# Round 0's gathered rows passed through TensorE into PSUM, its queries moved within a turn, and the last chunk of a round stored in pieces

## What is computed

```python
e   = relu((x[dst] - x[src]) @ theta_w.T + theta_b + x[src] @ phi_w.T + phi_b)
x   = layernorm(x + segment_max(e, dst))            # empty nodes: 0
hv  = x @ W_in + b_in
for W, b in ((W_u0, b_u0), (W_u1, b_u1)):
    m  = relu(concat(hv[src], he) @ W + b)
    hv = where(has_in, segment_max(m, dst) + hv, hv)
out = layernorm(x + relu(hv @ W_ro + b_ro))
```

## Time and profile before

| what | value |
|---|---|
| median of 3 runs | 3306.88 us (3306.12 to 3308.51) |
| the profiled execution | 3308.03 us |
| its span, first to last instruction | 3306.2 us |
| busy: POOL / PE / DVE / ACT | 2416.1 / 2101.3 / 1463.1 / 186.1 us |
| mean granted clock of TensorE | 0.831 of full speed (full: 2.4 GHz) |
| DMA | 770.03 MB, mean 233 GB/s |

### The profile page before, as it was taken

One profiled execution on the slowest core, in us unless ns is written; L12 is line 12 of the kernel. 1 busy time (PEld: TensorE's weight loads), 2 busy tenths in 40 slices (PEclk: granted clock), 3 DMA queues, 4 the chain that ended last, 5 costly groups with the idle time before them and its releaser, 6 DMA issues.

```text
span 3306.2 us, 21987 instructions
## 1 busy us (share of the span) xinstructions
PE 2101.3 (64%) x5442; PEld 1052.2 (32%) x5442; DVE 1463.1 (44%) x3430; ACT 186.1 (6%) x422; POOL 2416.1 (73%) x2536
## 2 busy tenths in 40 slices
PE   5322221222221888788787887778888888888867
PEld 4211111111110633333333333353343344333435
DVE  2655555555554733333333333323333333333337
ACT  1000000000000600000000000010000000000005
POOL 4777777777776677777777777667777777777765
PEclk8655555555555999999999999989999999999999
DMA  7666666666665767777777777677777777777764
GB/s 255 209 215 224 224 223 224 224 225 220 211 217 193 235 221 245 247 241 239 244 242 245 239 249 246 220 252 243 246 245 251 254 247 246 248 259 245 245 209 151
DMA packets 265661, 770.03 MB, mean 233 GB/s; under 512 B 55443, under 2 KB 114686, under 8 KB 227902
## 3 DMA queue, kind: packets, MB, share of 16 engines
q0 software_dynamic: 122208, 334.92, 33.5%
q1 hardware_dynamic: 84478, 354.64, 28.4%
q10 hardware_dynamic: 58848, 79.06, 8.0%
HBM read 421.22 MB, written 347.19 MB: 232 GB/s over the span
## 4 chain that ended last, share of the span: by engine, by line
POOL 47%; DMA 17%; issue 16%; PE 15%; DVE 3%; ACT 1%; DVEq 0%; ACTq 0%; POOLq 0%; SPq 0%
POOL gath L525 45%; DMA gath<-table,src_sb 16%; PE edge_ps L746 6%; PE edge_ps L744 4%; PE side_ps L685 2%; POOL gath L552 2%; PE edge_ps L685 2%; DVE hist L356 1%; DMA gath<-runs,end_row 1%; DVE hist L393 1%; ACT gath L636 0%; DMA runs<-hist 0%; ACT hist L623 0%; ACT x_sb L636 0%; DMA table<-hist 0%
## 5 line engine op out<-in xcount | busy, mean ns | idle before, releaser
L525 POOL DMA_INDIRECT gath<-table,src_sb x2352 | 2244.4, 954 | 767.0 <-issue 668.8
L356 DVE SCALAR_TENSOR_TENSOR hist<-hist,lift,edge_ps 128x256 f32<-128x256 f32 x1568 | 752.7, 480 | 1229.5 <-PE edge_ps L746 1167.9
L746 PE MATMUL edge_ps<-gath,ident 128*128 128x512 f32 x1568 | 852.3, 626 | 343.0 <-DMA gath<-table,src_sb 342.3
L744 PE MATMUL edge_ps<-w_e,he_sb 128*128 128x512 f32 x1568 | 817.7, 603 | 1.0 <-DVE hist L416 0.5
L693 PE MATMUL edge_ps<-dst_f,onehot 128*128 128x512 f32 x200 | 145.5, 881 | 731.9 <-DVE onehot L281 731.9
L356 DVE SCALAR_TENSOR_TENSOR hist<-hist,lift,gath 128x256 f32<-128x256 f32 x784 | 381.2, 486 | 426.1 <-DMA gath<-table,src_sb 382.5
L746 PEld LDWEIGHTS edge_ps<-gath,ident 128*128 128x128 f32 x1568 | 284.1, 194 | 808.4 <-DMA gath<-table,src_sb 553.3
L744 PEld LDWEIGHTS edge_ps<-w_e,he_sb 128*128 128x128 f32 x1568 | 298.5, 196 | 349.4 <-issue 333.9
L693 PEld LDWEIGHTS edge_ps<-dst_f,onehot 128*128 128x128 f32 x200 | 57.7, 318 | 809.4 <-DVE onehot L281 759.0
L595 ACT COPY hv_sb<-side_ps 128x256 f32<-128x256 f32 x147 | 54.7, 372 | 2884.0 <-PE edge_ps L746 1865.1
L552 POOL DMA_INDIRECT gath<-runs,end_row x147 | 151.7, 1032 | 49.0 <-issue 43.6
(11 more groups left out here) (125 smaller groups left out, 904.9 us busy)
## 6 DMA issues: line engine op xcount, KB each, us to landing
runs<-hist SPq DMA_DIRECT2D x294, 1024.0 KB, 5.2
he_sb<-in_he ACTq DMA_DIRECT2D x196, 256.0 KB, 3.0
gath<-table,src_sb POOLq DMA_INDIRECT x2352, 3.3
table<-hist SPq DMA_DIRECT2D x72, 256.0 KB, 3.5
back_T<-x1T ACTq DMA_DIRECT2D x98, 128.0 KB, 3.3
back_T<-in_xT ACTq DMA_DIRECT2D x49, 128.0 KB, 2.5
x_sb<-in_x SPq DMA_DIRECT2D x49, 128.0 KB, 4.9
back_T<-msgT ACTq DMA_DIRECT2D x49, 128.0 KB, 5.8
```

The costliest lines, as they stand in the source:

```text
L356: state = V.scalar_tensor_tensor(hist[:, s % H, :], hist[:, (s - 1) % H, :], lift[:, t:t + 1], edges, ALU.add, ALU.max)
L525: pool.indirect_dma_start(gath[:, s % G, :], None, tables[r], bass.IndirectOffsetOnAxis(src_sb[:, t:t + 1], 0)).then_inc(gathered[s % G // ...
L744: T.matmul(bank, he_sb[:, c % NHE, at:at + P], w_e[r - 1][:, :], start=True, stop=False)
L746: last = T.matmul(bank, ident[:, :], flat(gath[:, s % G:s % G + 2, :]), start=False, stop=True)
```

## The change

- **Rows through PE.** A new function `first_rows` takes the place of PE's round 0 loop. For each pair of steps PE waits for both gathers and multiplies the rows with the identity into one PSUM bank. DVE reads from the bank in all rounds. Round 0 uses three banks (0 to 2), so PE is at most 6 steps ahead of DVE; rounds 1 and 2 keep six.
- **Ring release.** In round 0 POOL's wait for a free slot of `gath` is now on `group_summed` (PE) instead of `state_done` (DVE).
- **Queries early.** `pick_rows` moves from step 8 of a turn to step 0, PE's `pick` stands after the second group, `find_ends` after step 7 instead of after step 15. `back` stands after the third group. `multiply_weights` stands after the sixth group of turn 1 and uses the two query banks and a side bank; `weights_and_biases` stands ahead of step 32 instead of behind step 47.
- **Store in pieces.** The last chunk of each round goes out as four DMAs of two steps (256 KB) instead of one of eight (1 MB). `stores(n)` counts the DMAs of a chunk's slot.

```diff
-EDGE_BANKS = 6
+EDGE_BANKS = (3, 6, 6)
+WEIGHTS_AT = (LATE_TURN + 1) * BODY
+        weights_ps = [edge_ps[:, BANKS, :], edge_ps[:, BANKS + 1, :], side_ps[:, 0, :]]
+        edge_bank = lambda r, t: edge_ps[:, t // 2 % EDGE_BANKS[r], :]
+        def stores(n):
+            return sum(SC // GS if m % CHUNKS == CHUNKS - 1 else 1 for m in range(n % NS, n + 1, NS))
             def edge_maxima(r):
-                    if r == 0 and t % BODY == BODY // 2:
+                    if r == 0 and t == WEIGHTS_AT:
+                        weights_and_biases()
+                    if r == 0 and t % BODY == 0:
                         pick_rows(col_no[:, :])
                     if s % SC == 0 and s >= H:
-                        dve.wait_ge(stored[s // SC % NS], 16 * (s // H))
-                    if r == 0 and s % 2 == 0:
-                        dve.wait_ge(gathered[s % G // 2], 2 * 16 * (s // G + 1))
-                    elif r > 0 and s % GS == 0:
-                        dve.wait_ge(group_summed, s // GS - GROUPS + 1)
+                        dve.wait_ge(stored[s // SC % NS], 16 * stores(s // SC - NS))
+                    if s % GS == 0:
+                        dve.wait_ge(group_summed, s // GS + 1)
                     V.drain()
-                    edges = gath[:, s % G, :] if r == 0 else edge_ps[:, bank, half:half + D]
+                    edges = edge_bank(r, t)[:, t % 2 * D:(t % 2 + 1) * D]
...
-                    if r == 0 and t % BODY == BODY - 1:
+                    if r == 0 and t % BODY == BODY // 2 - 1:
...
-                        if i == LATE_TURN + 1:
-                            weights_and_biases()
             def store_runs(r):
-                    sp.wait_ge(state_done, (n + 1) * SC // GS)
-                    at = n % NS * SC
-                    sp.dma_start(runs_by_part[:, c * SC:(c + 1) * SC, :], hist[:, at:at + SC, :]).then_inc(stored[n % NS], 16)
+                    piece = GS if c == CHUNKS - 1 else SC
+                    for t in range(c * SC, (c + 1) * SC, piece):
+                        s = r * STEPS + t
+                        sp.wait_ge(state_done, (s + piece) // GS)
+                        sp.dma_start(runs_by_part[:, t:t + piece, :], hist[:, s % H:s % H + piece, :]
+                                     ).then_inc(stored[n % NS], 16)
             def gather_edges(r):
-                    if s % GS == 0 and G <= s < STEPS + G:
-                        pool.wait_ge(state_done, (s - G) // GS + 1)
-                    elif s % GS == 0 and s >= G:
-                        pool.wait_ge(group_summed, (s - G) // GS - GROUPS + 1)
+                    if s % GS == 0 and s >= G:
+                        pool.wait_ge(group_summed, (s - G) // GS + 1)
+            def first_rows():
+                for g in range(GROUPS):
+                    turn_no, at = g // (BODY // GS), g % (BODY // GS) * GS
+                    if g == 0:
+                        pe.wait_ge(product_out, NU)
+                    if g * GS >= 2 * EDGE_BANKS[0]:
+                        pe.wait_ge(state_done, g - 2 * EDGE_BANKS[0] // GS + 1)
+                    for t in range(g * GS, (g + 1) * GS, 2):
+                        pe.wait_ge(gathered[t % G // 2], 2 * 16 * (t // G + 1))
+                        last = T.matmul(edge_bank(0, t), ident[:, :], flat(gath[:, t % G:t % G + 2, :]),
+                                        start=True, stop=True)
+                    last.then_inc(group_summed, 1)
+                    if at == GS:
+                        pick(turn_no + 1)
+                    if at == BODY // 4:
+                        for t in back_tiles(0, turn_no):
+                            back(t)
+                    if turn_no == LATE_TURN and at == BODY // 2 + GS:
+                        multiply_weights()
...
                 if r == 0:
-                    for i in range(TURNS):
-                        for t in back_tiles(0, i):
-                            back(t)
-                        pick(i + 1)
-                        if i == LATE_TURN:
-                            multiply_weights()
+                    first_rows()
```

More of the change, by code:

```diff
@@ L133, in gnn_kernel @@
         assert 2 * XT_BUFS <= G and 2 * (ROW_BUFS + UNIT_BUFS) <= G and 4 * UNIT_BUFS <= H
-        edge_ps = ctx.enter_context(nc.psum_tensor("edge_ps", [P, EDGE_BANKS, 2 * D], f32))
+        edge_ps = ctx.enter_context(nc.psum_tensor("edge_ps", [P, max(EDGE_BANKS), 2 * D], f32))
         side_ps = ctx.enter_context(nc.psum_tensor("side_ps", [P, 2, 2 * D], f32))
@@ L319, in weights_and_biases @@
                 dve.wait_ge(weights_mult, 1)
-                for n, w in enumerate((w_in_n0, w_in_n1, w_in_ro)):
-                    V.tensor_copy(flat(w[:, :, :]), edge_ps[:, n, :])
+                for w, w_ps in zip((w_in_n0, w_in_n1, w_in_ro), weights_ps):
+                    V.tensor_copy(flat(w[:, :, :]), w_ps)
                 for n, b_ps in ((NEXT0, edge_ps[:, 3, 0:D]), (NEXT1, edge_ps[:, 3, D:]), (OUT, side_ps[:, 1, 0:D])):
@@ L344, in edge_maxima @@
                     s = r * STEPS + t
-                    if r == 0 and t % BODY == BODY // 2:
+                    if r == 0 and t == WEIGHTS_AT:
+                        weights_and_biases()
+                    if r == 0 and t % BODY == 0:
                         pick_rows(col_no[:, :])
                     if s % SC == 0 and s >= H:
-                        dve.wait_ge(stored[s // SC % NS], 16 * (s // H))
-                    if r == 0 and s % 2 == 0:
-                        dve.wait_ge(gathered[s % G // 2], 2 * 16 * (s // G + 1))
-                    elif r > 0 and s % GS == 0:
-                        dve.wait_ge(group_summed, s // GS - GROUPS + 1)
+                        dve.wait_ge(stored[s // SC % NS], 16 * stores(s // SC - NS))
+                    if s % GS == 0:
+                        dve.wait_ge(group_summed, s // GS + 1)
                     V.drain()
-                    bank, half = s // 2 % EDGE_BANKS, s % 2 * D
-                    edges = gath[:, s % G, :] if r == 0 else edge_ps[:, bank, half:half + D]
+                    edges = edge_bank(r, t)[:, t % 2 * D:(t % 2 + 1) * D]
                     state = V.scalar_tensor_tensor(hist[:, s % H, :], hist[:, (s - 1) % H, :], lift[:, t:t + 1], edges,
@@ L530, in join_partitions @@
                 for n in range((r + 1) * CHUNKS - NS, (r + 1) * CHUNKS):
-                    pool.wait_ge(stored[n % NS], 16 * (n // NS + 1))
+                    pool.wait_ge(stored[n % NS], 16 * stores(n))
                 if r == 0:
@@ L580, in load_he @@
                 if n >= NHE:
-                    act.wait_ge(group_summed, (n - NHE + 1) * HC // GS)
+                    act.wait_ge(group_summed, GROUPS + (n - NHE + 1) * HC // GS)
                 act.dma_start(he_sb[:, n % NHE, :], a["he"][:, c * HC // 2 * P:(c + 1) * HC // 2 * P]
@@ L724, in multiply_weights @@
                         for h in range(KH):
-                            T.matmul(edge_ps[:, n, m * D:(m + 1) * D], w_inT[:, h, m * P:(m + 1) * P], w[:, h, :],
+                            T.matmul(weights_ps[n][:, m * D:(m + 1) * D], w_inT[:, h, m * P:(m + 1) * P], w[:, h, :],
                                      start=(h == 0), stop=(h == KH - 1))
@@ L737, in messages @@
                         pe.wait_ge(he_loaded[c % NHE], 16 * (c // NHE + 1))
[L738 to L742, removed]
+                    if g * GS >= 2 * EDGE_BANKS[r]:
+                        pe.wait_ge(state_done, r * GROUPS + g - 2 * EDGE_BANKS[r] // GS + 1)
+                    for t in range(g * GS, (g + 1) * GS, 2):
+                        s = r * STEPS + t
+                        bank = edge_bank(r, t)
                         at = s % HC // 2 * P
```

## The result

| | before | after |
|---|---|---|
| median | 3307.7 us (4 runs, 3306.12 to 3310.69) | 3293.44 us (4 runs, 3290.11 to 3294.62) |
| ratio | | 0.9949, 95% interval 0.9937 to 0.9961 |
| span of the profiled execution | 3306.2 us | 3291.9 us |

The change makes the kernel 14.3 us faster, by 0.51%. The forecast was 20.6 us less. The time lies inside the stated range, outside the forecast's own range of 3281 to 3291 us. The direction and the main term are right; 6.3 us of the forecast gain are not there.

A forecast was written before the change was run, and what follows sets the result against it. POOL's issuing of gathers was taken to bound the kernel. The terms −18.4 + 1.5 − 4.6 + 0.9 = −20.6 us took 3306.88 to 3286.3 us; stated range 3280 to 3298 us, the forecast's own 3281 to 3291 us.

The forecast's parts named there:

- the main term: Round 0's gathering stretch: reading rows from PSUM instead of SBUF ends the stretching of POOL's gathers, gaining 18.4 us.
- What bounds the kernel: The three gathering stretches: POOL's issue sets the pace, 784 gathers at 1.25 us each; other engines only keep up.
- Rows through PE, −18.4 us: Round 0's stretch: without DVE's two-SBUF scan, POOL loses its 20.9 us excess except 1.5 and 1.0 us.
- The biases: Splitting of the biases in round 0: two gathers beside it stay stretched, keeping 1.5 us of the excess.
- the queries: DVE's query work once a turn in round 0, also with two SBUF inputs: keeps 1.0 us of the excess.
- PE's load, cost 0: Round 0's stretch: PE needs at most 18.5 us a turn against 20.0 us of gathers, so keeps up.
- Rival C: Round 0's PE queue: at 1.2 GHz a turn lasts 21.0 us and holds POOL up, 3335 us; chance 0.05.
- The lump of weights in turns 1 to 3, cost 0: PE and DVE weight and bias work delays PE about 30 us, under the 45 us that would hold POOL.
- full blocking: A gather meeting DVE's two-SBUF instruction would lose up to its whole length; 0.18 us beside 0.55 us scans seemed to disagree.
- The store itself, −4.6 us: Round ends: the last store is 256 KB instead of 1 MB, 2.4 us each, saving 1.4 + 1.8 + 1.4 us.
- the tail, +1.5 us for PE in round 0: Round 0's end: one new PE step between the last pair's landing and DVE's scan adds 1.5 us.
- +0.3 us a round for pieces that delay the last gathers: Round ends: pieces sent while the last gathers land might delay those, 0.3 us each round, 0.9 us in all.

The follow-up runs named there:

- The added instructions: Changed kernel plus one DVE instruction behind each round 0 scan, with two SBUF tensors or a tensor_scalar: 3860.99 and 3849.46 us, POOL busy 755.9 and 745.2 us in round 0.

## Why the prediction was partly right, by its steps

- **What bounds the kernel.** Right on the chip of the result: 784 issues of 1.25 us per round, unchanged. On the other four chips delivery of the gathers bounds each round, which nothing in the trace of before hinted at.
- **Rows through PE, −18.4 us.** Right in mechanism and size: −18.7 us in the stretch. The added instructions showed the cause. The biases kept 1.6 us (1.5 forecast), the queries and everything else 0.7 us (1.0). Two readings on the way were wrong. ACT is not busier in round 1 than in round 0 (18.23 against 19.51 us), so that did not rule it out. And the 0.18 us lost beside a scan of 0.55 us was taken to speak against full blocking; it is what full blocking gives, as the gather started with 0.31 us of that scan left, less the 0.13 us.
- **PE's load, cost 0.** Right: POOL never idled over its issue gap, the clock rose to 0.83. Rival C did not come near.
- **The lump of weights in turns 1 to 3, cost 0.** Right, no idle of POOL there.
- **The store itself, −4.6 us.** Right in direction, a little low: 1.84, 1.74 and 1.83 us saved, −5.4 us.
- **The step that failed: the tail, +1.5 us for PE in round 0 and +0.3 us a round for pieces that delay the last gathers.** Together 2.4 us were forecast; it measured 10.5 us, of which 8.9 us is PE's part (1.5 forecast) and 1.5 us later landings (0.9 forecast). I priced the tail as that of the last pair, one PE step behind a landing, at a clock between the two levels, and took rounds 1 and 2 for unchanged. At all three ends there were two pairs behind the landing, at a granted clock of 0.50, 0.63 and 0.62. The clock alone is 5.2 us. At the end of round 2, where before and after have the same gather and the same six matmuls in the chain, it is 1.70 of the 1.84 us.
- **What causes the lateness.** That stays open. The small stores may have slowed gathers that were under way, but each gather in the chain was issued ahead of the first of them. A rival that the forecast did not have is the other traffic: in round 0 the four loads of edge features and the 1 MB store of the chunk before now go out close ahead of the last gathers, and in round 1 that store went out 1.9 us earlier than before, beside the last pair but one. No experiment ran on a chip where gathers come in time. A kernel with the rows through PE and the whole store is what would tell the two apart there; I would now expect it about 5 us slower than the changed one if the pieces are not the reason, and within 2 us of it if they are.

Where the gain goes on the slow chips is shown: it is off the critical path. The same 18 us leave POOL's busy time (762.0 to 743.6), and turn into waiting for ring slots and a longer backlog.

## What to carry to other kernels

An engine that only issues DMAs can be slowed by another engine's choice of operands. Compare the duration of its instruction between stages that differ in what the other engines read, minimum and median against maximum and sum; moving one operand to PSUM was worth 18.7 us here, for an extra matmul step per pair of steps that cost nothing within the stretch. Then lay the stretched instructions against the ends of the other engine's, not against their lengths: a constant distance, 0.82 us here, tells waiting from slow sharing. At the end of a pipelined stretch price not the last item but the last few, and at the clock that an engine has after it ran dry: cutting the final store in four took 1.8 us off it each time, and PE's part ahead of it grew by 1.7 to 3.8 us. And look at what else a moved instruction takes along, as `back` took the loads behind it. And check on more than one chip what bounds the kernel, if you can: a gain on the pace-setter is worth nothing where another resource sets the pace.

## What the runs showed of the hardware

- Five chips, one program: 3307 us on one, 3818 to 3840 us on four others, with the same issue time of a gather (0.946 to 0.949 us) on all. On the four, 784 gathers of 128 rows of 1 KB took 1107 to 1122 us in rounds 1 and 2 whether 207 or 132 GB/s moved. That it is the chip, and not another condition of these runs, is not shown.
- A gather instruction that meets a DVE instruction with two tensors in SBUF ends 0.82 us after it (117 of the 123 gathers over 1 us in round 0 before, and 67 beside the added instruction), and so does one that meets a float32 `tensor_scalar` of 128x256 from SBUF to SBUF (43 gathers). A scan of 0.48 us stretched it by up to 0.26 us, 784 scans by 18.6 us in sum, 784 such `tensor_scalar` by 2.8 us. A 128x1024 float32 `tensor_tensor` of 1.23 us, with a cast behind it, cost 0.8 us; there too the gathers ended 0.88 us after it. With the scan's second tensor in PSUM, 1568 gathers of rounds 1 and 2 stayed under 0.97 us. The Trainium skill, "SBUF — State Buffer", section "Who interferes with whom", has the second to issue fully blocked until the first is done. These runs agree: the constant 0.82 us from the end of DVE's instruction is that wait.
- TensorE, after 2.2 to 3.2 us without work at the three ends of rounds, had a granted clock of 0.50 to 0.63 and did a pair of steps in up to 1.71 us, the lower of its two levels (1.2 and 2.4 GHz); after 0.72 us idle, in the earlier trace rows, and after 1.66 us idle at the end of round 2 before, in 1.13 us at 1.00.
